# Softmax maxima of the graph attention passes: cut into three bfloat16 parts and picked with bfloat16 one-hots

## The chip, the cores and the metric

One core of one Trainium2 chip runs the whole program. The metric is the device time of one execution in microseconds (us), the lower the better. TensorE (PE; its weight loads are listed apart as PEld) multiplies, VectorE (DVE) and ScalarE (ACT) do elementwise work, GpSimd (POOL) issues the indirect gathers, and SyncE (SP) issues the plain transfers.

## What is computed

The reference runs four graph networks over the same 3,125 nodes and 103,125 edges, each followed by a residual and a layer norm. The change touches only the third, a diffusion network with three graph attention ("gat") layers. Cut to what matters:

```
for gw, a_s, a_d, gb, aw, ab, g, b in layers:          # 3 layers, 8 heads, width 256, 256, 128
    xw     = (x @ gw).reshape(n, 8, c)
    al_s   = einsum(xw, a_s);  al_d = einsum(xw, a_d)   # per node and head
    logits = leaky_relu(al_s[src] + al_d[dst], 0.2)
    m      = segment_max(logits, dst)                   # per node and head
    e      = exp(logits - m[dst])
    out    = segment_sum(e / segment_sum(e, dst)[dst] * xw[src], dst)
```

## The kernel before

**Tiling.** The edges are sorted by destination and cut into groups of 512 edges that share one block of 128 destination nodes. Two groups make a step: 8 items (`BATCH`) of 128 edges. A gat layer is one `gat_pass` of 114 steps, so there are 342 steps in three layers. Each engine runs its own loop over the steps, four steps to a turn of the loop (`pipeline`); a pair such as `(2, logits)` says that a part works two steps behind. Nothing but this list sets the order on an engine, and semaphores join the engines.

**One step, in the order of its data.** POOL gathers the source rows of the step's edges with 8 indirect transfers (L681); its gather of step n waits for the messages of step n-4. ACT takes al_s out of them (`pack`), PE transposes it (`turn`, L1795), DVE scans for the running maxima of each run of equal destinations (`scan`, L1683), and PE transposes back (`turn_back`, L1801). DVE's `run_ends` (L1690) keeps the maxima at the end of each run and zeros the rest, and ACT puts the flag of a run's end beside them. PE's `pick` (L1811) multiplies these 9 columns by the one-hot matrix of the edges' destinations, one matmul for each of 8 items, in float32: since each destination has one run in an item, the product picks its maximum. DVE's `maxima` (L1700 to L1729) makes the new maximum of each node of the block, cuts it into three bfloat16 parts whose sum is the float32 number, and PE's `dst_gather` (L1824) brings al_d and the maximum to the edges with 24 bfloat16 matmuls of 16 columns (8 items by 3 parts). This document calls that group the burst. DVE's `logits` (L1735, L1738, L1741) and ACT's `power` (L1669) make the exponentials, DVE's `messages` (L1748) multiplies the gathered rows by them, PE's `sums` (L1834, in two halves, float32) adds up the messages by destination, and DVE's `add` (L1768, L1772) adds them to the accumulator.

**Around the change.** The one-hots arrive from memory in bfloat16 (`hot_half`, a ring of 4 that SP loads, L709), and ACT widens them to float32 (`hot`, L719); `pick` and `sums` read the float32 ones. DVE's list for a turn is `maxima` (two behind), `scan` (one behind), `logits` (two), `run_ends` (one), `keep_fade` (two), `add(0)` (three), `messages` (two), `add(1)` (three). So DVE reaches the messages of one step only after `run_ends` of the next. PE's list is `turn` (one), `sums(0)` (three), `dst_gather` (two), `turn_back` (one), `sums(1)` (three), `pick` (one).

## Time and profile before

| | before |
|---|---|
| Median of 3 runs | 11818.08 us (11797.62 to 11822.92) |
| Time of the profiled execution | 11901.01 us |
| Its span, first to last instruction | 11899.2 us |
| Busy: PE, PEld | 6783.1 us (57%), 5699.3 us (48%) |
| Busy: POOL, DVE, ACT | 6085.0 (51%), 4232.3 (36%), 1966.8 us (17%) |
| Mean granted TensorE clock | 0.616 of full speed |
| gat layers 0, 1, 2 (first to last L1735) | 4617.5 to 6426.2, 6554.9 to 8354.9, 8481.9 to 10191.6 us |

The profiled execution took 83 us (0.7%) more than the median of the plain runs, and every duration below is from it. No engine is busy for 60% of the span. The three gat passes are 5.3 of the 11.9 ms.

In a timeline row the first number is the start in us from the span's start and the second the length; then come engine, line, operation, what it writes and reads, and the number of instructions that are merged in the row. In brackets stands the idle time of the engine just before it and what ended it; "remote" and "issue" mean that the profile names no instruction. One float32 matmul of the program is two MATMUL records, a bfloat16 one is one.

### The profile page before, as it was taken

What the parts mean: (1) busy time and instruction counts of PE and PEld (TensorE: products, weight loads), DVE (VectorE), ACT (ScalarE), POOL (GpSimd) and SP (SyncE); (2) the same over time, 40 slices, a digit from 0 to 9 for tenths busy, and PEclk for the clock granted to TensorE, in tenths of its full rate; (3) what the DMA queues carried; (4) which work ended last, traced back from release to release, by engine and by line L of the source; (5) the groups of instructions that cost most, each with busy time, mean ns of one, the idle gap of its engine ahead of it and who ended that gap; (6) DMA issues with size and microseconds to landing.
All of it is one profiled execution on the core that took longest, in us unless ns stands there. A gap on an engine that the chain in (4) does not pass through costs nothing. (4 is left out here: it accounts for less than half of the span.)

```text
span 11899.2 us, 136950 instructions
## 1 busy us (share of the span) xinstructions
PE 6783.1 (57%) x37299; PEld 5699.3 (48%) x37300; DVE 4232.3 (36%) x12350; ACT 1966.8 (17%) x5277; POOL 6085.0 (51%) x6396
## 2 busy tenths in 40 slices
PE   3554555556444445666666666676555555545454
PEld 3554544455322324555555555555455555444444
DVE  4333322222211113444444444444334333333333
ACT  1222200001211121111112111111211111111111
POOL 4666656665466653444443444444344444355554
PEclk6555556555667666666666666666655555566566
DMA  4444423232233322333332333333222222233333
GB/s 122 142 140 137 134 68 78 76 78 63 73 73 74 74 70 88 103 103 103 103 103 87 103 104 104 104 104 102 63 74 76 75 75 75 60 95 95 96 94 83
DMA packets 774628, 1092.78 MB, mean 92 GB/s; under 512 B 389184, under 2 KB 429440, under 8 KB 774160
## 3 DMA queue, kind: packets, MB, share of 16 engines
q0 software_dynamic: 233760, 503.07, 17.3%
q1 hardware_dynamic: 540784, 588.70, 16.5%
q8 instruction: 40, 0.66, 0.0%
q14 instruction: 44, 0.36, 0.0%
HBM read 1016.16 MB, written 75.04 MB: 92 GB/s over the span
## 5 line engine op out<-in xcount | busy, mean ns | idle before, releaser
L681 POOL DMA_INDIRECT gat_rows<-xw_table,gat_index x2736 | 2592.0, 947 | 3118.1 <-DVE gat_msg_s L1748 1971.9
L1834 PE MATMUL bank<-gat_msg_s,gat_hot 128*128 128x264 f32 (+1 forms) x5472 | 1942.7, 528 | 28.6 <-DVE gat_msg_s L1748 16.3
L1811 PE MATMUL bank<-gat_ends_s,gat_hot 128*128 128x9 f32 x5472 | 1153.2, 350 | 1183.1 <-issue 857.8
L1811 PEld LDWEIGHTS bank<-gat_ends_s,gat_hot 128*128 128x128 f32 x5472 | 1137.0, 316 | 1319.8 <-issue 950.0
L1834 PEld LDWEIGHTS bank<-gat_msg_s,gat_hot 128*128 128x128 f32 x5472 | 1430.8, 303 | 296.3 <-issue 31.0
L681 POOL DMA_INDIRECT att_rows<-pre_table,att_index x912 | 862.5, 946 | 830.1 <-ACT att_index L671 478.9
L681 POOL DMA_INDIRECT msg_rows<-pre_table,msg_index x912 | 864.8, 948 | 651.0 <-ACT msg_index L671 385.1
L681 POOL DMA_INDIRECT gcn_rows<-in_x,gcn_index x912 | 878.6, 963 | 573.8 <-ACT gcn_index L671 291.1
L681 POOL DMA_INDIRECT gcn_rows<-x_table,gcn_index x912 | 883.4, 969 | 554.4 <-issue 278.9
L893 PE MATMUL bank<-gcn_rel,gcn_rhot 100*128 100x64 f32 x3648 | 705.7, 347 | 792.4 <-issue 608.1
L730 PE MATMUL bank<-gcn_msg_s,gcn_hot 128*128 128x128 f32 x3648 | 844.9, 379 | 538.0 <-issue 530.4
L893 PEld LDWEIGHTS bank<-gcn_rel,gcn_rhot 100*128 100x128 f32 x3648 | 682.9, 271 | 821.9 <-issue 758.2
L730 PEld LDWEIGHTS bank<-gcn_msg_s,gcn_hot 128*128 128x128 f32 x3648 | 728.1, 281 | 620.8 <-issue 619.6
L1735 DVE TENSOR_TENSOR gat_lg<-gat_al_s,bank 128x64 f32<-128x64 f32 x342 | 75.7, 221 | 1957.9 <-remote 1924.1
L1748 DVE TENSOR_TENSOR gat_msg_s<-gat_rows,bank 128x2112 f32<-128x2112 f32 (+1 forms) x342 | 681.3, 1992 | 0.4
L1824 PE MATMUL bank<-gat_parts,gat_dhot 128*128 128x16 bf16 x8208 | 265.2, 172 | 687.8 <-DVE gat_parts L1729 386.0
L1824 PEld LDWEIGHTS bank<-gat_parts,gat_dhot 128*128 128x128 bf16 x8208 | 243.9, 101 | 857.5 <-issue 856.7
L1259 PE MATMUL bank<-msg_w,msg_attr_t 128*128 128x512 f32 x456 | 346.6, 903 | 397.0 <-ACT msg_attr_t L1169 231.9
L1205 DVE TENSOR_TENSOR msg_pre_s<-msg_rows,bank 128x512 f32<-128x512 f32 x228 | 146.5, 684 | 1167.0 <-DMA gcn_hot_half<-edge_hots 1051.7
L861 DVE TENSOR_TENSOR bank<-gcn_rows,bank 128x512 f32<-128x512 f32 x228 | 157.6, 691 | 1101.8 <-remote 720.6
L1669 ACT ACTIVATE bank<-gat_lg 128x64 f32<-128x64 f32 x342 | 77.9, 228 | 2485.6 <-DVE gat_lg L1741 1841.6
L730 PE MATMUL bank<-msg_msg_s,msg_hot 128*128 128x129 f32 x1824 | 288.5, 301 | 309.9 <-issue 309.5
(279 smaller groups left out, 8925.6 us busy)
## 6 DMA issues: line engine op xcount, KB each, us to landing
gcn_ids<-rel_rows SPq DMA_DIRECT2D x228, 400.0 KB
gat_hot_half<-edge_hots SPq DMA_DIRECT2D x342, 256.0 KB
gat_dhot<-dst_hots SPq DMA_DIRECT2D x342, 256.0 KB
gcn_dst<-dst_rows SPq DMA_DIRECT2D x114, 512.0 KB
gat_rows<-xw_table,gat_index POOLq DMA_INDIRECT x2736
edge_hots<-gcn_hot_half SPq DMA_DIRECT2D x114, 256.0 KB
dst_hots<-gcn_dhot SPq DMA_DIRECT2D x114, 256.0 KB
gcn_hot_half<-edge_hots SPq DMA_DIRECT2D x114, 256.0 KB
```

The lines of the kernel that those rows point to most:

```text
L681: pool.indirect_dma_start(self.rows[n.q][:, j, :], None, self.table, bass.IndirectOffsetOnAxis(ap=self.index[n.q][:, j:j + 1], axis=0))\
L730: ins = pe.matmul(place(banks, g, width), hot[:, g * GROUP + j, :], msg[:, g * GROUP + j, 0:width], start=j == 0, stop=j == GROUP - 1)
L861: dve.tensor_tensor(comp[q], g.rows[n.q][:, :, :], rel_ps[q][:, :].rearrange("p (b d) -> p b d", b=BATCH), ALU.mult)\
L893: ins = pe.matmul(rel_ps[q][:, j * DIM:(j + 1) * DIM], rhot[q][:, j * P:(j + 1) * P], rel[:, :], start=True, stop=True)
L1205: ins = dve.tensor_tensor(pre[q][:, part, :], g.rows[n.q][:, part, :], edge_ps[q][i][:, :].rearrange("p (j d) -> p j d", j=GROUP), ALU.add)
L1259: ins = pe.matmul(edge_ps[q][i][:, :], attr_t[q][:, i * P:(i + 1) * P], w[:, :], start=True, stop=True)
L1669: act.activation(powers, lg[q][:, :, :], ACT.Exp).then_inc(powered, 1)
L1735: dve.tensor_tensor(lg[q][:, :, :], al_s[q][:, :, :], drow[:, :, 0:HEADS], ALU.add)\
L1748: dve.tensor_tensor(msg[q][:, :, :].rearrange("p b (h e) -> p b h e", h=HEADS), rows[n.q][:, :, 0:wide].rearrange("p b (h e) -> p b h e", ...
L1811: ins = pe.matmul(pick_ps[:, j * (HEADS + 1):(j + 1) * (HEADS + 1)], hot[n.q][:, j, :], ends[q][:, j, :], start=True, stop=True)
L1824: ins = pe.matmul(row_ps[:, j * size:(j + 1) * size], dhot[n.q][:, j * P:(j + 1) * P], parts[q][:, j // GROUP, k, :], start=k == 0, stop=k ...
L1834: ins = pe.matmul(sum_ps[g][:, 0:wide], hot[n.q][:, g * GROUP + j, :], msg[q][:, g * GROUP + j, :], start=j == 0, stop=j == GROUP - 1)
```

## The change

`run_ends` is followed on DVE by a new part, `cut_ends`, which cuts the 9 columns of the run ends (8 maxima and the flag) into three bfloat16 parts whose sum is the float32 number. The first part needs no instruction: it is the upper half of each float32 word, read in place. `pick` then makes three bfloat16 matmuls for each item, with the bfloat16 one-hots as they came from memory, and adds them up in PSUM. It no longer waits for ACT's widening, but for the one-hots' landing and for the cut. SP's load of new one-hots now also waits until the pick four steps before is done, and the presets of the semaphore `picked` go from 2 to 4 with the waits shifted to match.

```diff
@@ scalar and vector
-                    dve.wait_ge(picked, n.total(1, 1))
+                    dve.wait_ge(picked, n.total(1, RING - TWO + 1))
                     dve.tensor_tensor(ends[q][:, :, 0:HEADS], back_ps[:, 0:ROWS].rearrange("p (b h) -> p b h", b=BATCH),
                                       spread(m.run_end[:, n.items()], HEADS), ALU.mult).then_inc(masked, 1)
+
+                def cut_ends(n):
+                    q = n.of(TWO)
+                    dve.wait_ge(masked, n.total(1, 2))
+                    dve.wait_ge(flagged, n.total(1, 1))
+                    dve.tensor_tensor(ends_rest[q][:, :, :], ends[q][:, :, :], upper(ends[q][:, :, :]), ALU.subtract).then_inc(ends_cut, 1)
+                    dve.wait_ge(ends_cut, n.total(1, 1))
+                    dve.tensor_tensor(ends_low[q][:, :, :], ends_rest[q][:, :, :], upper(ends_rest[q][:, :, :]), ALU.subtract)\
+                        .then_inc(ends_parted, 1)
...
-                pipeline(dve, (2, maxima), (1, scan), (2, logits), (1, run_ends), (2, keep_fade), (3, add(0)), (2, messages),
+                pipeline(dve, (2, maxima), (1, scan), (2, logits), (1, run_ends), (1, cut_ends), (2, keep_fade), (3, add(0)), (2, messages),
                          (3, add(1)))
@@ tensor
-                    hots.wait(pe, n)
-                    pe.wait_ge(masked, n.total(1, 2))
-                    pe.wait_ge(flagged, n.total(1, 1))
+                    pe.wait_ge(hots.hot_in[n.q], n.count(16, 16))
+                    pe.wait_ge(ends_parted, n.total(1, 1))
                     pe.wait_ge(offered, n.total(1, 1))
+                    pieces = upper(ends[q][:, :, :]), upper(ends_rest[q][:, :, :]), ends_low[q]
                     for j in range(BATCH):
-                        ins = pe.matmul(pick_ps[:, j * (HEADS + 1):(j + 1) * (HEADS + 1)], hot[n.q][:, j, :], ends[q][:, j, :],
-                                        start=True, stop=True)
+                        for k, piece in enumerate(pieces):
+                            ins = pe.matmul(pick_ps[:, j * (HEADS + 1):(j + 1) * (HEADS + 1)], hots.half[n.q][:, j, :], piece[:, j, :],
+                                            start=k == 0, stop=k == PARTS - 1)
                     ins.then_inc(picked, 1)
@@ sync
-                pipeline(sp, (0, hots.load(sp)), (0, load_runs), (0, load_dhot))
+                def load_hots(n):
+                    sp.wait_ge(picked, n.total(1, 1))
+                    hots.load(sp)(n)
+
+                pipeline(sp, (0, load_hots), (0, load_runs), (0, load_dhot))
```

On DVE, between the logits and the messages of a step inside the loop of layer 0, stands before the change:

```order
L1735 TENSOR_TENSOR gat_lg<-gat_al_s,bank 128x64
L1738 SCALAR_TENSOR_TENSOR gat_lg<-gat_lg 128x64
L1741 TENSOR_TENSOR gat_lg<-gat_lg,bank 128x64
L1690 ISA
L1690 TENSOR_TENSOR gat_ends_s<-bank,run_end 128x8x8
L1756 COPY bank<-gat_fade 128x16
L1768 ISA
L1768 TENSOR_TENSOR acc<-acc,bank 128x264
L1770 REGISTER_ALU
L1772 TENSOR_TENSOR acc<-acc,bank 128x264
L1748 TENSOR_TENSOR gat_msg_s<-gat_rows,bank 128x2112
```

And at the same place of the changed kernel, whose line numbers are some 6 to 16 higher (L1750 is `logits`, L1696 `run_ends`, L1763 `messages`):

```order
L1750 TENSOR_TENSOR gat_lg<-gat_al_s,bank 128x64
L1753 SCALAR_TENSOR_TENSOR gat_lg<-gat_lg 128x64
L1756 TENSOR_TENSOR gat_lg<-gat_lg,bank 128x64
L1696 ISA
L1696 TENSOR_TENSOR gat_ends_s<-bank,run_end 128x8x8
L1703 TENSOR_TENSOR gat_ends_rest<-gat_ends_s 128x72
L1705 TENSOR_TENSOR gat_ends_low<-gat_ends_rest 128x72
L1771 COPY bank<-gat_fade 128x16
L1783 ISA
L1783 TENSOR_TENSOR acc<-acc,bank 128x264
L1785 REGISTER_ALU
L1787 TENSOR_TENSOR acc<-acc,bank 128x264
```

The two subtractions over 72 elements a partition (L1703, L1705) are new; the rest keeps its order.

On PE, the end of a step in the loop of layer 0 and the start of the next, before the change:

```order
L1824 MATMUL bank<-gat_parts,gat_dhot 128x16 x24
L1799 REGISTER_ALU
L1801 MATMUL bank<-ident,gat_run_max 128x64
L1832 REGISTER_ALU
L1834 MATMUL bank<-gat_msg_s,gat_hot 128x264 x4
L1807 REGISTER_ALU
L1811 MATMUL bank<-gat_ends_s,gat_hot 128x9 x8
L1795 MATMUL bank<-ident,gat_al_s 64x128
```

In the changed kernel the eight float32 matmuls of L1811 are 24 bfloat16 ones (L1827); the first six of them, behind the sums:

```order
L1850 MATMUL bank<-gat_msg_s,gat_hot 128x264 x4
L1827 MATMUL bank<-gat_ends_s,gat_hot_half 128x9
L1827 MATMUL bank<-gat_ends_rest,gat_hot_half 128x9
L1827 MATMUL bank<-gat_ends_low,gat_hot_half 128x9
L1827 MATMUL bank<-gat_ends_s,gat_hot_half 128x9
L1827 MATMUL bank<-gat_ends_rest,gat_hot_half 128x9
L1827 MATMUL bank<-gat_ends_low,gat_hot_half 128x9
```

Their place among the other groups of PE is the same.

## Rows read from the trace of the kernel before

**Rows 1.** Groups of the page: busy, mean ns | idle before, releaser.

```profile
L1811 PE MATMUL bank<-gat_ends_s,gat_hot 128*128 128x9 f32 x5472 | 1153.2, 350 | 1183.1 <-issue 857.8
...
L1735 DVE TENSOR_TENSOR gat_lg<-gat_al_s,bank 128x64 f32<-128x64 f32 x342 | 75.7, 221 | 1957.9 <-remote 1924.1
```

**Rows 2.** Line L1735 in gat layers 0 and 2.

```profile
L1735 DVE TENSOR_TENSOR gat_lg<-gat_al_s,bank x114: 220/222/222, 4617.5 to 6426.2; 128x64 f32<-128x64 f32 x114
...
L1735 DVE TENSOR_TENSOR gat_lg<-gat_al_s,bank x114: 220/222/223, 8481.9 to 10191.6; 128x64 f32<-128x64 f32 x114
```

**Rows 3.** Timeline, one step, layer 0: start, length, engine, line [idle, releaser].

```profile
5216.64 0.22 DVE L1735 TENSOR_TENSOR gat_lg<-gat_al_s,bank 128x64 f32<-128x64 f32 x1 [7.00 <-remote]
5216.90 0.23 DVE L1738 SCALAR_TENSOR_TENSOR gat_lg<-gat_lg 128x64 f32<-128x64 f32 x1
...
5217.35 0.23 DVE L1690 TENSOR_TENSOR gat_ends_s<-bank,run_end 128x64 f32<-128x64 f32 x1
...
5217.67 3.56 PE L1811 MATMUL bank<-gat_ends_s,gat_hot 128*128 128x9 f32 x16 [3.88 <-issue]
...
5218.48 2.35 DVE L1748 TENSOR_TENSOR gat_msg_s<-gat_rows,bank 128x2112 f32<-128x2112 f32 x1
...
5221.27 3.73 PE L1834 MATMUL bank<-gat_msg_s,gat_hot 128*128 128x264 f32 x8
5221.60 0.95 POOL L681 DMA_INDIRECT gat_rows<-xw_table,gat_index  x1 [6.71 <-DVE gat_msg_s L1748]
...
5226.10 0.75 PE L1824 MATMUL bank<-gat_parts,gat_dhot 128*128 128x16 bf16 x24 [1.09 <-issue]
...
5230.36 0.94 POOL L681 DMA_INDIRECT gat_rows<-xw_table,gat_index  x1 [0.30 <-issue]
...
5233.12 0.22 DVE L1735 TENSOR_TENSOR gat_lg<-gat_al_s,bank 128x64 f32<-128x64 f32 x1 [6.70 <-remote]
```

**Rows 4.** Timeline, another step of layer 0.

```profile
5463.70 0.95 POOL L681 DMA_INDIRECT gat_rows<-xw_table,gat_index  x1 [6.69 <-DVE gat_msg_s L1748]
...
5467.14 0.76 PE L1824 MATMUL bank<-gat_parts,gat_dhot 128*128 128x16 bf16 x24
...
5472.48 0.95 POOL L681 DMA_INDIRECT gat_rows<-xw_table,gat_index  x1 [0.30 <-issue]
...
5473.73 0.22 DVE L1735 TENSOR_TENSOR gat_lg<-gat_al_s,bank 128x64 f32<-128x64 f32 x1 [6.51 <-remote]
```

**Rows 5.** Timeline, one step of layer 2.

```profile
9096.73 0.95 POOL L681 DMA_INDIRECT gat_rows<-xw_table,gat_index  x1 [5.40 <-DVE gat_msg_s L1748]
...
9097.73 0.17 DVE L1700 TENSOR_SCALAR gat_pen<-bank 128x8 f32<-128x8 f32 x1 [1.17 <-PE bank L1811]
...
9101.08 0.79 PE L1824 MATMUL bank<-gat_parts,gat_dhot 128*128 128x16 bf16 x24 [1.32 <-issue]
...
9105.49 0.95 POOL L681 DMA_INDIRECT gat_rows<-xw_table,gat_index  x1 [0.30 <-issue]
...
9108.28 0.22 DVE L1735 TENSOR_TENSOR gat_lg<-gat_al_s,bank 128x64 f32<-128x64 f32 x1 [7.16 <-remote]
```

**Rows 6.** What L1700 waited for, us and times: layer 0, then layer 2.

```profile
  PE bank L1811: 18.0, 11
...
  PE bank L1811: 138.0, 104
```

**Rows 7.** Timeline, layer 0: a burst with no gather under way.

```profile
5585.86 0.79 PE L1824 MATMUL bank<-gat_parts,gat_dhot 128*128 128x16 bf16 x24 [12.81 <-DVE gat_parts L1729]
...
5586.69 0.22 DVE L1735 TENSOR_TENSOR gat_lg<-gat_al_s,bank 128x64 f32<-128x64 f32 x1 [0.75 <-PE bank L1824]
```

**Rows 8.** Attention pass: its bfloat16 burst, and the windows view of it.

```profile
10819.13 1.49 PE L2133 MATMUL bank<-q_parts,att_dhot 128*128 x24
...
10820.75 0.69 DVE L2073 TENSOR_TENSOR att_prod<-att_rows,bank 128x512 f32<-128x512 f32 x1 [0.67 <-PE bank L2133]
...
10819.10:10820.70 1.60, 1.60 (x28) 1.57 (x26) 0.70 (x1) 0.00 (x0) 0.94 (x1) 0.50 0.65 178
```

More of the change, by code:

```diff
@@ L1595, in gat_pass @@
         turned, scanned, backed, masked, flagged, picked = (st.sem(s) for s in ("turned", "scanned", "backed", "masked", "flagged", "picked"))
+        ends_cut, ends_parted = st.sem("ends_cut"), st.sem("ends_parted")
         penal, offered, best, shown, sloped, local = (st.sem(s) for s in ("penal", "offered", "best", "shown", "sloped", "local"))
@@ L1603, in gat_pass @@
         runs, run_max = ring_sb(st, "runs", RING, [ROWS, P]), ring_sb(st, "run_max", TWO, [ROWS, P])
-        ends = ring_sb(st, "ends_s", TWO, [P, BATCH, HEADS + 1])
+        ends, ends_rest = (ring_sb(st, s, TWO, [P, BATCH, HEADS + 1]) for s in ("ends_s", "ends_rest"))
+        ends_low = ring_sb(st, "ends_low", TWO, [P, BATCH, HEADS + 1], BF16)
         pen, cand = ring_sb(st, "pen", TWO, [P, BATCH]), ring_sb(st, "cand", TWO, [P, BATCH, HEADS])
@@ L1649, in bring @@
                     ins.then_inc(shown, 1)
-                    act.wait_ge(picked, n.total(1, 1))
+                    act.wait_ge(picked, n.total(1, RING - TWO + 1))
                     act.activation(ends[q][:, :, HEADS:HEADS + 1], m.run_end[:, n.items()].unsqueeze(2), ACT.Copy).then_inc(flagged, 1)
@@ L1698, in maxima @@
                     earlier[:], ids = ids[:-PAIR], ids[-PAIR:]
-                    dve.wait_ge(picked, n.total(1, TWO + 1))
+                    dve.wait_ge(picked, n.total(1, RING + 1))
                     dve.tensor_scalar(pen[q][:, :].unsqueeze(2), view[:, :, HEADS:HEADS + 1], -1.0, -FAR, ALU.add, ALU.mult)\
@@ L1840, in _ @@
                 pe.sem_inc(backed, TWO)
-                pe.sem_inc(picked, TWO)
+                pe.sem_inc(picked, RING)
                 pe.sem_inc(dst_rows, RING)
```

## The prediction

> **What bounds the kernel now.** I read the groups of the page first, to see what waits. `logits` (L1735) on DVE waits 1957.9 us over 342 steps, 1924.1 of it for "remote", a releaser that the profile cannot name [rows 1]. `pick` (L1811), which the change rebuilds, is busy for 1153.2 us on PE [rows 1]: much work, but work on an engine that is idle four tenths of the time. So the question is whether any wait ends with it.
>
> The steps of the three layers are compared by the first and last start of L1735: 113 intervals in (6426.2 − 4617.5) / 113 = 16.01 us in layer 0 and (10191.6 − 8481.9) / 113 = 15.13 us in layer 2 [rows 2].
>
> Then the timeline of one step [rows 3]. L1735 starts at 5216.64 (call it R), the messages at 5218.48 and end at 5220.83. POOL, which waited for them, starts its first gather at 5221.60, 0.77 later, and ends the eighth at 5230.36 + 0.94 = 5231.30. The next L1735 starts at 5233.12. The loop is logits, run ends, add, messages, eight gathers, logits: 1.84 + 2.35 + 0.77 + 9.70 + 1.82 = 16.48 us. DVE has hardly a gap between L1735 and L1748, so that is a chain of DVE work, without cover.
>
> Why do logits wait for the gathers? They need only `dst_gather` (L1824, the burst), which is recorded from 5226.10 to 5226.85, 6.3 us before they start [rows 3]. In another step, where the burst starts 5467.14 − 5463.70 = 3.44 us after the first gather, logits start 5473.73 − 5473.43 = 0.30 after the end of the last one [rows 4]. In rows 3 it starts 4.50 after the first gather and logits come 1.82 after the last. In layer 2 it is 9101.08 − 9096.73 = 4.35, and 9108.28 − 9106.44 = 1.84 [rows 5]. With no gather under way a burst ending at 5586.65 releases logits at 5586.69 [rows 7]; and in the attention pass a burst of the same 24 matmuls, 1.49 us long, hands on at once while the DMA engines are 65% busy [rows 8]. I read this so: a completion of PE's that falls late enough among the gathers is seen only when they have drained, and 0.30 or 1.8 us behind the last is decided by where the burst starts, with the border between 3.44 and 4.35 us after the first gather. That is an inference from few rows; the sum rests on it.
>
> `pick` runs from R + 1.03 to R + 4.59, before the first gather at R + 4.96 [rows 3]. What reads it is L1700, the start of the maxima. It waits for the pick in 11 steps of layer 0, 18.0 us in all, but in 104 steps of layer 2, 138.0 us [rows 6]: there the messages are half as wide, so DVE arrives before PE.
>
> **The change, part by part.** *Added on DVE's path: two subtractions a step.* Each depends on the one before it. L1735 and L1738 are such a pair, of 64 elements, and start 0.26 apart [rows 3]; for 72 elements I take the same. So 2 × 0.26 = 0.52 us a step, 342 steps, **+178 us**. The next instruction keeps its distance, and messages, gathers and logits all start 0.52 later: nothing covers it. Lower bound: the 0.17 us that the smallest operation lasts (L1700, rows 5), 2 × 0.17 × 342 = +116. Upper bound: a hand-over between engines, 5217.67 − 5217.35 = 0.32 from L1690 to the pick [rows 3], 2 × 0.32 × 342 = +219. I stay near the pair of dependent operations, the same kind of thing.
>
> *Taken from PE: the pick.* Sixteen float32 records take 3.56 us; 24 bfloat16 ones take 0.75 in the burst of the same step [rows 3]. The new pick starts after two cuts, at about R + 1.5, and ends near R + 2.3, some 2.3 us earlier. In layers 0 and 1 it ends before DVE is done with the messages (R + 4.19) either way, or nearly: only the 18.0 us of waits can go [rows 6], and I allow as much again for layer 1. Between 0 and −36, taken **−20 us**. PE's sums start 5221.27 after the old pick's end at 5221.23; they may now start 0.4 earlier, but PE then idles 1.09 before the burst in any case [rows 3]: nothing.
>
> In layer 2 the wait of L1700 was 1.17 in rows 5. Of it some 0.2 would remain between two dependent starts of DVE, so the maxima and the burst come about 0.96 earlier, at 9100.12, 3.39 after the first gather instead of 4.35. That is just on the early side of the one early row I have (3.44), so the release may go from 1.84 to 0.30 behind the last gather, 1.54 a step. None of 114 steps gives 0, all give −176. As the new place is so near the border, and as not all of the 138.0 us need be gone (a wait of DVE's own may stand behind it), I take half: 57 × 1.54 = **−88 us**. A step that stays late gains nothing, since its release hangs on the last gather.
>
> *Moved.* The pick no longer waits for ACT's widening, but for the one-hots' landing four steps ahead; SP's load of one-hots waits for the pick of four steps before instead of for the widening. Behind it in SP's queue stand the loads of runs and of the destination one-hots. The latter already waits for `dst_rows`, that is, for a burst that is seen as late as logits see it, so the added wait, for an earlier event of an earlier step, ends first: 0. The flag of ACT, a step old by then: 0.
>
> Sum: 178 − 20 − 88 = **+70 us** against the profiled execution's 11901.01; scaled by 11818.08 / 11901.01 it is +70 again on the median, **11,888 us**. Bounds: 116 − 36 − 176 = −96 and +219, so 11,722 to 12,037.
>
> **A colder TensorE?** PE's granted clock is 0.50, its lower level of 1.2 GHz, beside the short attention burst [rows 8], and the sums of rows 3 take 3.73 us and still end at 5225.00, 1.09 before the burst. So a PE that is half as fast in its sums costs nothing there. The Trainium skill, "TensorE: Matmul & The Clock Gate", section "HAM oscillation — how this bites in real kernels", says that gaps in TensorE's work send it back to half rate, which speaks against making PE idler; the rows agree that PE works at half rate here and give no cost for it.
>
> **The rivals.**
> *A, faster.* Every step of layer 2 falls on the early side. Place: the start of the burst after the first gather; it decides from the border on, if that is at 3.4 us or above. Then −176, and with all 36 us and cuts at 0.21 (+145): −67, **11,750 us**. For it: 3.39 is below 3.44. Against: by 0.05, and only if nothing else delays L1700. Chance 0.28.
> *B, no change.* The cuts near 0.26 and layer 2 nearly all early, or the cuts lighter and half of it early: 150 − 150, **11,818 us**. Also here: the cuts turn out to be covered, which would need a gap in DVE's chain from R to the messages, and I see none. Chance 0.20.
> *C, far slower.* A completion of the pick itself, now a burst of bfloat16 matmuls, is held like the other until the gathers are over, and the maxima with it. It would need the pick to fall among the gathers; it ends 2.6 us before them. In irregular steps it might: a step then grows by up to a further round of about 5 us (half the 9.70 of the gathers), in one of ten steps 34 × 5 = +170, and with the cuts **12,150 us**. Or the sums grow past their margin of 1.09. Chance 0.08.
> *The forecast:* cuts in full, layer 2 partly repaid: 11,845 to 12,000. Chance 0.44.
>
> **How the numbers follow.** ±0.2% of 11818, that is 11,794 to 11,842, is about what a measurement of this kernel can tell from no change. Slower: forecast and C, 0.52. Within: B, 0.20. Faster: A, 0.28. The predicted time is the forecast's, 11,888. Its own range is 11,845 to 12,000. The whole range, 11,730 to 12,010, leaves out C (0.08), the cuts at their upper bound with no repayment (some 0.06) and the last of A (0.05).
>
> **What would show it.** The starts of the two cuts (L1703, L1705) 0.26 apart, and messages (L1763) 2.36 after L1750 in layer 0 rather than 1.84. L1827 as 24 records in about 0.8 us, ended before the first gather. L1715 in layer 2 with hardly a wait for PE. L1840 there at 3.4 us after the first gather in all steps, and L1750 at 0.30 behind the last gather in half of them, 1.8 in the other half. Mean steps of 16.01 + 0.52 − 0.1 = 16.4 in layer 0 and 15.13 + 0.52 − 0.77 = 14.9 us in layer 2. Wrong it would be if the release did not depend on the burst's place: then no −88, and 11,976. And if the earlier pick moved more than L1700, as when the order of POOL's gathers relative to the burst changes in layers 0 and 1 as well, where each step that turns early gives 1.5 us, 228 steps up to 350.

## The result and the profile after

The changed kernel took 11904.87 us (median of 4 runs, 11880.46 to 11928.7), the kernel before on the same chip 11815.43 us. The ratio is 1.0082, 95% interval 1.0065 to 1.0099: slower, by 77 to 117 us. The forecast was 11,888 us, +70.

The groups of the page of the changed kernel that answer to [rows 1]:

```profile
L1827 PE MATMUL bank<-gat_ends_s,gat_hot_half 128*128 128x9 bf16 x2736 | 250.6, 169 | 1289.2 <-issue 1289.2
...
L1750 DVE TENSOR_TENSOR gat_lg<-gat_al_s,bank 128x64 f32<-128x64 f32 x342 | 75.7, 221 | 1897.2 <-remote 1836.4
```

There are three such groups of L1827. Their matmuls overlap in time, so their busy times are not to be added: together they cover 269 us, where L1811 took 1153.2. TensorE as a whole is busy 805 us less (5978.4 against 6783.1). The wait of the logits for "remote" is 1836.4 us, 88 less than before. So 805 us of work left the engine, and the kernel became slower.

Line L1750 in gat layers 0 and 2 (first and last start), beside [rows 2]:

```profile
L1750 DVE TENSOR_TENSOR gat_lg<-gat_al_s,bank x114: 220/222/223, 4577.5 to 6397.6; 128x64 f32<-128x64 f32 x114
...
L1750 DVE TENSOR_TENSOR gat_lg<-gat_al_s,bank x114: 220/222/223, 8482.5 to 10193.6; 128x64 f32<-128x64 f32 x114
```

(6397.6 - 4577.5) / 113 = 16.11 us a step in layer 0, and 15.14 in layer 2. The prediction had put 16.4 and 14.9 there. The profile of before is very likely of an execution on a slower chip (see "The kernel before again" below), so small differences to [rows 2] are not to be read by themselves.

The timeline of one step of layer 0, changed kernel, beside [rows 3]. Of the 24 rows of the pick the first and the last are shown:

```profile
5305.68 0.22 DVE L1750 TENSOR_TENSOR gat_lg<-gat_al_s,bank 128x64 f32<-128x64 f32 x1 [6.38 <-remote]
...
5306.38 0.22 DVE L1696 TENSOR_TENSOR gat_ends_s<-bank,run_end 128x64 f32<-128x64 f32 x1
5306.64 0.23 DVE L1703 TENSOR_TENSOR gat_ends_rest<-gat_ends_s 128x72 f32<-128x72 f32 x1
5306.91 0.23 DVE L1705 TENSOR_TENSOR gat_ends_low<-gat_ends_rest 128x72 bf16<-128x72 f32 x1
5307.24 0.17 PE L1827 MATMUL bank<-gat_ends_s,gat_hot_half 128*128 128x9 bf16 x1 [2.81 <-issue]
...
5307.83 0.17 PE L1827 MATMUL bank<-gat_ends_low,gat_hot_half 128*128 128x9 bf16 x1
5308.01 2.35 DVE L1763 TENSOR_TENSOR gat_msg_s<-gat_rows,bank 128x2112 f32<-128x2112 f32 x1
...
5311.14 0.94 POOL L681 DMA_INDIRECT gat_rows<-xw_table,gat_index  x1 [5.63 <-DVE gat_msg_s L1763]
...
5315.64 0.75 PE L1840 MATMUL bank<-gat_parts,gat_dhot 128*128 128x16 bf16 x24 [1.26 <-issue]
...
5319.90 0.95 POOL L681 DMA_INDIRECT gat_rows<-xw_table,gat_index  x1 [0.30 <-issue]
5322.42 0.34 SPq L1635 DMA_DIRECT2D gat_dhot<-dst_hots  x1
5322.43 0.22 DVE L1750 TENSOR_TENSOR gat_lg<-gat_al_s,bank 128x64 f32<-128x64 f32 x1 [6.47 <-remote]
```

The cuts stand 0.27 apart and behind `run_ends`; the messages start 2.33 after L1750, not 1.84. The pick takes 0.76 us and is over before the messages start. The burst is 4.50 behind the first gather and the logits 5322.43 - 5320.85 = 1.58 behind the last one. So messages and gathers take over the whole 0.5 us. The step as a whole is 0.27 us longer than the one in [rows 3] (16.75 against 16.48), since there the logits came 1.82 behind the last gather.

The row of SyncE (SPq, L1635) bears on the main open point. SyncE's load of new destination one-hots waits for the same semaphore (`dst_rows`) as the logits, and it goes on at 5322.42, 0.01 us before them, 6.03 us behind the burst's recorded end (5316.39). Two engines see it late at the same moment, so it is the completion that comes late, and VectorE is not what delays it.

The same rows in layer 2, for a step with an early burst, beside [rows 5]:

```profile
9097.99 0.95 POOL L681 DMA_INDIRECT gat_rows<-xw_table,gat_index  x1 [5.87 <-DVE gat_msg_s L1763]
9098.03 0.17 DVE L1715 TENSOR_SCALAR gat_pen<-bank 128x8 f32<-128x8 f32 x1 [0.21 <-issue]
...
9101.32 0.79 PE L1840 MATMUL bank<-gat_parts,gat_dhot 128*128 128x16 bf16 x24 [1.79 <-DVE gat_parts L1744]
...
9106.75 0.94 POOL L681 DMA_INDIRECT gat_rows<-xw_table,gat_index  x1 [0.30 <-issue]
9108.81 0.22 DVE L1750 TENSOR_TENSOR gat_lg<-gat_al_s,bank 128x64 f32<-128x64 f32 x1 [7.42 <-remote]
```

What L1715, the start of the maxima, waited for in layer 2, in us and times, beside [rows 6]:

```profile
  DMA edge_hots<-gcn_hot_half: 68.1, 9
  issue: 62.8, 101
```

In the regular steps the wait for the pick is gone: 62.8 us remain in 101 steps, where it was 138.0 in 104. The burst is 9101.32 - 9097.99 = 3.33 us behind the first gather, as forecast (3.39), but the logits follow the last gather's end by 9108.81 - 9107.69 = 1.12 us, not 0.30.

The other nine waits are of another kind, and the releaser that the profile names for them is not a fitting one, since L1715 waits for the semaphore `picked` alone. About once in twelve steps the gathers of two steps stand close together, in layer 2 fifteen in a row, and the pick falls among them. One of the nine:

```profile
8844.06 0.17 DVE L1715 TENSOR_SCALAR gat_pen<-bank 128x8 f32<-128x8 f32 x1 [8.26 <-DMA edge_hots<-gcn_hot_half]
```

The pick had ended at 8828.00 by its record, 16.06 us earlier, with gathers running until 8841.21. So this is rival C of the prediction, in irregular steps. Over all three layers the maxima's idle time grew from 443.3 to 473.7 us, though its part for the pick (164.1 us before) is gone; the part with the unfitting name rose from 120.7 to 311.2. It did not cost time of its own: such a pair of steps took 10.8 + 21.7 = 32.5 or 12.2 + 20.4 = 32.6 us in layer 2 before, and takes 9.8 + 22.7 = 32.5 now. The kernel before had the same pairs, and there the longest wait stood at L1772 (10.79 us for "remote" in one of them).

For every step whose eight gathers stand in a row, the burst's start behind the first gather and the logits' start behind the end of the last can be counted from the same rows. Layer 2 has 92 such steps in each kernel:

| | burst behind first gather | steps | logits behind the last gather's end |
|---|---|---|---|
| before | 4.3 to 4.4 | 80 | 1.7 to 1.9 in 78, 0.3 and 1.0 in one each |
| before | 4.0, 4.2, 4.7, 5.6 | 12 | 1.7 to 1.8 in all |
| after | 3.3 to 3.4 | 45 | 1.0 to 1.1 in 22, 1.7 in 7, 0.3 in 6, before its end in 10 |
| after | 4.0 | 19 | 1.7 in 15, 0.2 to 1.0 in 4 |
| after | 4.5 | 27 | 1.7 to 1.9 in all |
| after | 2.5 | 1 | before its end |

On average the logits came 1.74 us behind the last gather before and come 1.08 behind it now. In layers 0 and 1 of the changed kernel a burst at 3.4 to 3.7 was released at 0.3 us behind the last gather or earlier in 88 of 90 steps, and one at 4.5 at 1.5 to 1.7 in all 52; at 4.1 to 4.2 both kinds stand side by side.

### The profile page after: what moved, and what is told of

It is laid out like the page before. It is cut to its first block and busy times, and to the rows that moved or that the text cites. A ratio compares the mean times of both kernels' runs of the same rounds, so it can differ in the third digit from the quotient of the medians.

```text
span 11878.7 us, 143529 instructions
## 1 busy us (share of the span) xinstructions
PE 5978.4 (50%) x40035; PEld 4797.1 (40%) x40036; DVE 4377.9 (37%) x13034; ACT 1967.9 (17%) x5277; POOL 6086.8 (51%) x6396
## 5 line engine op out<-in xcount | busy, mean ns | idle before, releaser
L1850 PE MATMUL bank<-gat_msg_s,gat_hot 128*128 128x264 f32 (+1 forms) x5472 | 2031.9, 541 | 628.4 <-DVE gat_msg_s L1763 479.7
L730 PE MATMUL bank<-gcn_msg_s,gcn_hot 128*128 128x128 f32 x3648 | 796.0, 369 | 421.3 <-issue 415.7
L1827 PE MATMUL bank<-gat_ends_s,gat_hot_half 128*128 128x9 bf16 x2736 | 250.6, 169 | 1289.2 <-issue 1289.2
L730 PEld LDWEIGHTS bank<-gcn_msg_s,gcn_hot 128*128 128x128 f32 x3648 | 695.3, 273 | 480.5 <-issue 480.1
L1827 PEld LDWEIGHTS bank<-gat_ends_s,gat_hot_half 128*128 128x128 bf16 x2736 | 230.2, 104 | 1425.1 <-issue 1422.5
L1750 DVE TENSOR_TENSOR gat_lg<-gat_al_s,bank 128x64 f32<-128x64 f32 x342 | 75.7, 221 | 1897.2 <-remote 1836.4
L1763 DVE TENSOR_TENSOR gat_msg_s<-gat_rows,bank 128x2112 f32<-128x2112 f32 (+1 forms) x342 | 681.4, 1992 | 0.2 <-issue 0.2
L1259 PE MATMUL bank<-msg_w,msg_attr_t 128*128 128x512 f32 x456 | 302.3, 799 | 457.6 <-ACT msg_attr_t L1169 353.4
L730 PE MATMUL bank<-att_msg_s,att_hot 128*128 128x64 f32 x1824 | 343.7, 344 | 178.8 <-issue 175.2
```

The lines of the kernel that those rows point to most:

```text
L730: ins = pe.matmul(place(banks, g, width), hot[:, g * GROUP + j, :], msg[:, g * GROUP + j, 0:width], start=j == 0, stop=j == GROUP - 1)
L1259: ins = pe.matmul(edge_ps[q][i][:, :], attr_t[q][:, i * P:(i + 1) * P], w[:, :], start=True, stop=True)
L1750: dve.tensor_tensor(lg[q][:, :, :], al_s[q][:, :, :], drow[:, :, 0:HEADS], ALU.add)\
L1763: dve.tensor_tensor(msg[q][:, :, :].rearrange("p b (h e) -> p b h e", h=HEADS), rows[n.q][:, :, 0:wide].rearrange("p b (h e) -> p b h e", ...
L1827: ins = pe.matmul(pick_ps[:, j * (HEADS + 1):(j + 1) * (HEADS + 1)], hots.half[n.q][:, j, :], piece[:, j, :], start=k == 0, stop=k == PART ...
L1850: ins = pe.matmul(sum_ps[g][:, 0:wide], hot[n.q][:, g * GROUP + j, :], msg[q][:, g * GROUP + j, :], start=j == 0, stop=j == GROUP - 1)
```

## The experiments

Each ratio is to the kernel before, run on the same chip. The runs did not all fall on one chip: on most the kernel before took 11,815 to 11,920 us, on one 8,795. Of the kernel before there are two profiles, and both are, the first very likely, from a chip where it takes about 11,920.

**One part alone: the cuts.** The kernel before with the two subtractions, which nobody reads:

```diff
-pipeline(dve, ..., (2, logits), (1, run_ends), (2, keep_fade), ...
+pipeline(dve, ..., (2, logits), (1, run_ends), (1, cut_ends), (2, keep_fade), ...
```

> The kernel before with the two subtractions added, their results read by nobody; the pick stays float32. My theory (two dependent DVE operations cost 2 x 0.26 us a step on the path, nothing comes back): 342 x 0.52 = +178 us, ratio 1.015 (1.012 to 1.018), slower than the changed kernel. Rival (a subtraction is cheap, and the changed kernel's +0.8% is all there is, the new pick giving nothing back): +90 us, ratio 1.008. Rival (half-step releases are a lottery that a shift of half a us can turn either way): anything from 1.00 to 1.02, with the starts of L1735 behind the last gather showing another mix of 0.3 and 1.8 us than in the kernel before.

Measured 1.0093 (1.0078 to 1.0109), 11923.98 against 11817.4 us: +107. The starts in layers 0 and 2:

```profile
L1746 DVE TENSOR_TENSOR gat_lg<-gat_al_s,bank x114: 220/221/223, 4586.9 to 6422.0; 128x64 f32<-128x64 f32 x114
...
L1746 DVE TENSOR_TENSOR gat_lg<-gat_al_s,bank x114: 220/221/222, 8518.8 to 10233.2; 128x64 f32<-128x64 f32 x114
```

That is 16.24 and 15.17 us a step. In layer 2 L1711, the maxima, still waits for the pick 104 times:

```profile
  PE bank L1822: 104.3, 104
```

The first theory (+178) misses. The +90 of the second lies within the interval, but its reason does not hold: the two subtractions stand 0.27 us apart here as well, and the pick does give something back (next run). The third, the mix of releases, is what is seen: in layer 2 the pick does not move with the cuts, only messages and gathers do, so the burst falls 3.8 to 4.0 us behind the first gather instead of 4.3, and 37 of 54 such steps are released at 0.1 to 0.3. The 0.5 us is nearly paid back there: the layer takes 1714.4 us, against 1709.7 and 1711.5 in the two profiles of the kernel before.

**The other part alone: the pick.** The changed kernel without the cuts; the pick multiplies the upper halves and twice a tile of zeros, which leaves out the lower bits of the maxima:

```diff
-                    pe.wait_ge(ends_parted, n.total(1, 1))
+                    pe.wait_ge(masked, n.total(1, 2))
+                    pe.wait_ge(flagged, n.total(1, 1))
-                    pieces = upper(ends[q][:, :, :]), upper(ends_rest[q][:, :, :]), ends_low[q]
+                    pieces = upper(ends[q][:, :, :]), none, none
```

> The changed kernel without the two subtractions: the pick is three bfloat16 matmuls an item, of the upper halves and of twice a tile of zeros, so the maxima lose their lower bits. My theory (the short pick lets the maxima of layer 2 start earlier, and some steps are then released 0.3 instead of 1.8 us behind the last gather): -60 to -180 us, ratio 0.985 to 0.995. Rival (the short pick gives nothing, the cut is worth only +90): ratio 1.000.

Measured 0.9977 (0.9968 to 0.9986): -25 us. It gains, but a quarter of what I had forecast. Against it the changed kernel is 112 us slower by the medians. Of the two profiled executions it is 92 us slower, and its three gat layers, first to last logits of each, are 5351.9 - 5239.2 = 113 us longer: all that the cuts cost lies there.

The two profiles also show how it splits. In layers 0 and 1 it is 29 and 30 us, 0.26 a step: the logits come on average 1.00 and 0.98 us behind the last gather in pick_only and 0.76 and 0.72 in the changed kernel, so a quarter of a us comes back by a better mix of releases. In layer 2 it is 53 us, 0.47 a step; there the mix gets a little worse (0.93, then 1.08). And the parts are not independent: on top of the cuts the short pick is worth 11923.98 - 11904.87 = 19 us, of which 3 us in layer 2, where the cuts alone had already won most of the early releases.

What is an early release worth? In layer 2 of pick_only the messages start 3.40 us behind the last gather's end where the logits came 1.5 to 1.9 behind it (31 steps), 2.79 where they came at 0.9 to 1.2 (27 steps), and 2.49 where they came at 0 to 0.4 (28 steps). So 0.6 and 0.9 us, not 1.54. One of the last kind:

```profile
8470.93 0.69 PE L1807 MATMUL bank<-ident,gat_run_max 64*128 64x64 f32 x2
8475.55 0.94 POOL L681 DMA_INDIRECT gat_rows<-xw_table,gat_index  x1 [0.30 <-issue]
8476.78 0.22 DVE L1740 TENSOR_TENSOR gat_lg<-gat_al_s,bank 128x64 f32<-128x64 f32 x1 [6.40 <-remote]
8478.34 0.23 DVE L1695 TENSOR_TENSOR gat_ends_s<-bank,run_end 128x64 f32<-128x64 f32 x1 [0.82 <-DMA msg_te_b<-in_L_gnn_te_b]
```

The logits (L1740) come 0.29 behind the last gather's end (8476.49). But `run_ends` (L1695), which stands between them and the messages, reads `turn_back` (L1807), which PE had ended at 8471.62, and it starts only 1.85 behind that gather. (The releaser that the profile names for it is not a tensor of this pass.) It waits over 0.3 us in 20 of those 28 steps and in none of the other 58. So here the burst's completion is early and the next one of PE is still late, and half of the gain is lost again.

**A wait more on POOL.** To test why the logits are late, the gathers are held back until the burst is done:

```diff
             for j in range(BATCH):
+                if after is not None and j == 0:
+                    pool.wait_ge(after, n.total(1, 2))
+                    pool.sem_inc(self.passed, 1)
...
-                gather.program(pool, msg_made)
+                gather.program(pool, msg_made, dst_rows)
```

> The changed kernel, whose POOL in the gat passes waits for one thing more: the gathers of a step start only when the burst (dst_gather) of the step three before has completed. My theory (a completion of PE's that falls among gathers is seen only when they have drained): gathers that start right behind one burst are over, or nearly, when the next one ends some 9.3 us later, so a step falls from 16 to between 10.3 and 12 us in all three layers: -1100 to -1950 us, ratio 0.84 to 0.91, though it only adds a wait. Rival (logits wait for the gathers themselves, or for their rows, or DMA is the bound): the gathers start 4 to 5 us later in each step and nothing is gained, ratio 1.00 to 1.13, steps of 16 to 20 us.

Measured 0.9894 (0.9879 to 0.9909), steps of 15.1 us. A step's timeline:

```profile
5287.20 0.95 POOL L684 DMA_INDIRECT gat_rows<-xw_table,gat_index  x1 [6.40 <-PE bank L1843]
...
5291.29 0.17 PE L1830 MATMUL bank<-gat_ends_low,gat_hot_half 128*128 128x9 bf16 x1
...
5295.96 0.95 POOL L684 DMA_INDIRECT gat_rows<-xw_table,gat_index  x1 [0.30 <-issue]
5297.13 0.17 DVE L1718 TENSOR_SCALAR gat_pen<-bank 128x8 f32<-128x8 f32 x1 [5.05 <-DMA edge_hots<-gcn_hot_half]
5300.47 0.79 PE L1843 MATMUL bank<-gat_parts,gat_dhot 128*128 128x16 bf16 x24 [6.43 <-DVE gat_parts L1747]
5301.30 0.22 DVE L1753 TENSOR_TENSOR gat_lg<-gat_al_s,bank 128x64 f32<-128x64 f32 x1 [0.66 <-PE bank L1843]
```

The logits now follow the burst at once (5301.26, 5301.30). But the pick, ended at 5291.46 among the gathers, is seen by the maxima at 5297.13, 0.22 behind the last gather's end. The wait has moved from the burst to the pick. That is rival C of the prediction, now in every regular step. So a wait more makes the kernel faster, by far less than the 1100 us expected: I had counted one completion of PE's, and there are two in a step that DVE waits for.

**The cuts behind the messages.** One entry of DVE's list is moved:

```diff
-(1, run_ends), (1, cut_ends), (2, keep_fade), (3, add(0)), (2, messages), (3, add(1))
+(1, run_ends), (2, keep_fade), (3, add(0)), (2, messages), (1, cut_ends), (3, add(1))
```

> The changed kernel with the two subtractions behind the messages in DVE's list. The messages come 0.52 us earlier again, the pick ends at about R + 5.5 in layers 0 and 1, with the first gather at R + 5.0. My theory (the cuts before the messages are what costs; a completion within the first 3 us of the gathers is not held): -100 to -180 us against the changed kernel, less what the maxima lose by waiting some 0.4 us for the pick: ratio to the kernel before 0.993 to 1.002. Rival C of the prediction (the completion of the bfloat16 pick is held like the burst's once it falls among the gathers): the maxima wait up to 9 us more, ratio 1.15 or more.

Measured 1.0127 (1.0111 to 1.0142), slower than the changed kernel, where I had expected 0.993 to 1.002. A step's timeline:

```profile
5321.97 0.22 DVE L1750 TENSOR_TENSOR gat_lg<-gat_al_s,bank 128x64 f32<-128x64 f32 x1 [6.27 <-remote]
...
5326.93 0.94 POOL L681 DMA_INDIRECT gat_rows<-xw_table,gat_index  x1 [7.06 <-DVE gat_msg_s L1763]
...
5327.28 0.17 PE L1827 MATMUL bank<-gat_ends_low,gat_hot_half 128*128 128x9 bf16 x1
...
5328.97 0.17 DVE L1715 TENSOR_SCALAR gat_pen<-bank 128x8 f32<-128x8 f32 x1 [1.50 <-PE bank L1827]
...
5332.28 0.75 PE L1840 MATMUL bank<-gat_parts,gat_dhot 128*128 128x16 bf16 x24 [1.06 <-issue]
...
5335.67 0.95 POOL L681 DMA_INDIRECT gat_rows<-xw_table,gat_index  x1 [0.30 <-issue]
5338.60 0.22 DVE L1750 TENSOR_TENSOR gat_lg<-gat_al_s,bank 128x64 f32<-128x64 f32 x1 [6.24 <-remote]
```

The messages start at R + 1.83, 0.5 us earlier, as meant. But the pick ends half a us into the gathers, the maxima (L1715) start 5328.97 - 5327.45 = 1.52 us behind its end, at R + 7.0, the burst falls 5.35 behind the first gather, and the logits come 1.98 behind the last gather instead of 0.2 to 1.6. So "early among the gathers is not held" is wrong too: it is late by 1.5 us (the median of each layer is 1.52 or 1.53), not by all of the gathers.

**The kernel before again,** for a second profile:

> The kernel before, unchanged, for a second profile of it, since the first is of an execution 0.7% above the median. If the layers differ only by how often a step is released 0.3 or 1.7 us behind the last gather: the three gat layers together some 50 us shorter than the 5318 us of the first profile, with the same kinds of steps in another mix. Rival (the first one lost its time outside the gat layers): the gat layers again 5318 us, the rest 80 us shorter.

On this chip it took 11919.64 us (median), and the gat layers 5347 us: neither expectation. Outside of the gat layers this profile has 6582 us and the first one 6581, while the profiles from chips where the kernel before takes 11,815 to 11,820 have 6513 to 6547, and the other three from this chip 6555 to 6571. So the first profile's 11901.01 is very likely of such a chip as this, and not of a slow execution.

**The same wait in the kernel before** (edit as in after_wait):

> The kernel before, whose gathers of a step start only behind the burst of the step three before, as in after_wait; the pick stays float32. My theory (a completion of PE's among running gathers is seen when they have drained; with this wait it is no longer the burst that is held but the pick): the pick is among the gathers either way, whether it takes 3.6 or 0.8 us, and is seen behind the last gather; steps of 14.4 to 16.3 us, the ratio to the kernel before 0.980 to 0.990, a little below after_wait by the two cuts. Rival (the pick is late in after_wait for another reason, and a float32 pick is later by its own 2.8 us): ratio 1.02 to 1.06.

Measured 0.9496 (0.948 to 0.9512), far below what I expected; steps of 14.2 and 13.6 us. The maxima wait for the pick here too, and often start at R + 9.4, before the last gather ends. With the float32 pick the wait takes 5.0% off its kernel, with the bfloat16 one 1.9% (0.9894 / 1.0082). The two ran on different chips. Why a pick that ends later is seen earlier is open.

**Two pauses instead of one.** Five gathers wait for the pick, three for the burst:

```diff
+            if first is not None:
+                pool.wait_ge(first, n.total(1, 2))
             pool.wait_ge(used, n.total(1, 1))
...
+                if rest is not None and j == 5:
+                    pool.wait_ge(rest, n.total(1, 2))
+                    pool.sem_inc(self.passed, 1)
```

> The changed kernel with the eight gathers of a step in two groups: five wait for the pick of the step three before (and for the messages, as now), three for the burst of that step. So POOL pauses at both places at which DVE waits for PE. My theory: the pick ends at R + 5.0, after the three gathers (R + 0.8 to R + 4.5) have drained, and is seen at once; the five gathers run from R + 5.6 to R + 11.8, and the burst, done at R + 9.7, is seen 0.2 to 1.7 behind them: steps of 12.0 to 13.5 us in place of 16, ratio 0.89 to 0.93. Rival (gathers only have to be done, wherever they stand; or a pause costs what it frees): steps of 15 to 17, ratio 0.97 to 1.03.

Measured 0.9303 (0.9288 to 0.9319), 11087.03 us: steps of 13.4 us. A step's timeline:

```profile
5328.16 0.22 DVE L1755 TENSOR_TENSOR gat_lg<-gat_al_s,bank 128x64 f32<-128x64 f32 x1 [4.45 <-remote]
...
5334.10 0.94 POOL L686 DMA_INDIRECT gat_rows<-xw_table,gat_index  x1 [1.74 <-DMA edge_hots<-gcn_hot_half]
5334.89 0.17 DVE L1720 TENSOR_SCALAR gat_pen<-bank 128x8 f32<-128x8 f32 x1 [1.18 <-issue]
...
5338.15 0.78 PE L1845 MATMUL bank<-gat_parts,gat_dhot 128*128 128x16 bf16 x24 [1.30 <-issue]
5339.10 0.94 POOL L686 DMA_INDIRECT gat_rows<-xw_table,gat_index  x1 [0.30 <-issue]
5341.59 0.22 DVE L1755 TENSOR_TENSOR gat_lg<-gat_al_s,bank 128x64 f32<-128x64 f32 x1 [3.17 <-remote]
```

The pick no longer delays the maxima, and the burst, done at 5338.93, is seen 1.55 behind the last gather's end. The long steps are gone too: none takes over 16.6 us, where the changed kernel has nine of 21 to 23 us in each layer. The work is that of the changed kernel, in 0.9303 / 1.0082 = 0.923 of its time: where the gathers stand decides. It beats both kernels.

**Pick first, additions one step later,** with the wait of after_wait (PE's list ends `(1, pick), (3, sums(1))`, DVE's has `(4, add(1)), (3, add(0))` ahead of the messages):

> As after_wait, and besides PE does the pick before the second half of the sums, and DVE does the second addition of a step one step later, before the first addition and the messages of the next. So the pick ends at R + 2.5, 1.7 us behind the start of the gathers, and the additions no longer stand before the maxima. My theory (only completions that fall late among the gathers are held): the pick is seen at once, the maxima start at R + 5.6, the burst ends at R + 9.7 and is seen 0.2 to 1.7 us behind the last gather's end at R + 10.5: steps of 10.7 to 12.3 us, ratio 0.85 to 0.90. Rival (every completion among gathers is held, early or late): the maxima start at R + 10.7 or later again, steps of 15 to 16, ratio 0.98 to 1.01.

Measured 0.9508 (0.9492 to 0.9524), steps of 14.2 and 13.9 us, between theory and rival. In its timeline the pick ends 1.7 us into the gathers, and the maxima start 6.9 us later:

```profile
5317.20 0.94 POOL L684 DMA_INDIRECT gat_rows<-xw_table,gat_index  x1 [5.84 <-PE bank L1844]
...
5318.73 0.17 PE L1831 MATMUL bank<-gat_ends_low,gat_hot_half 128*128 128x9 bf16 x1
...
5325.81 0.17 DVE L1722 TENSOR_SCALAR gat_pen<-bank 128x8 f32<-128x8 f32 x1 [3.41 <-DMA edge_hots<-gcn_hot_half]
5325.94 0.94 POOL L684 DMA_INDIRECT gat_rows<-xw_table,gat_index  x1 [0.30 <-issue]
```

The maxima started before the last gather had, so "only when they have drained" does not hold either.

**Plain copies for the gathers,** which leave out the gathering (the first 1024 rows of the table each time):

> The kernel before, whose eight indirect gathers of a gat step are eight plain copies of as many rows each (always the first 1024 rows of the table, so the gathered values are other ones), issued by POOL and waited for in the same places. If what delays PE's completions is the indirect gathers themselves: no burst is seen late any more, L1735 starts behind the burst, at some R + 9.3 to R + 10.5, ratio 0.80 to 0.88. Rival (it is the traffic of the rows, or of all transfers, 11 KB a partition and step, whoever describes it): PE's completions are late as before, ratio 0.97 to 1.02. Rival (POOL's issuing of any transfer is what holds them): the same as the second, with POOL busy as now.

This fell on the chip on which the kernel before takes 8794.81 us, and measured 0.9965 (0.9952 to 0.9977). A step's timeline:

```profile
4708.65 0.75 PE L1827 MATMUL bank<-gat_parts,gat_dhot 128*128 128x16 bf16 x24 [1.86 <-issue]
4709.44 0.22 DVE L1738 TENSOR_TENSOR gat_lg<-gat_al_s,bank 128x64 f32<-128x64 f32 x1 [0.46 <-PE bank L1827]
```

The logits follow the burst at once, steps are 10.2 us. But the kernel before, with its indirect gathers, is within 0.4% of it on this chip. The passes that the edit left alone, whose gathers are still indirect, show the same. In the first network (gcn) ACT's widening of the one-hots waits for PE's sums. The group of the page in the kernel before, and then here:

```profile
L719 ACT ACTIVATE gcn_hot<-gcn_hot_half 128x1024 f32<-128x1024 bf16 x114 | 120.6, 1058 | 1245.9 <-remote 1025.1 <-issue 115.8 <-PE bank L730 97.1
...
L722 ACT ACTIVATE gcn_hot<-gcn_hot_half 128x1024 f32<-128x1024 bf16 x114 | 120.4, 1057 | 1005.5 <-PE bank L733 996.6 <-DMA gcn_hot_half<-edge_hots 8.9
```

Here the widening starts 0.04 to 0.10 us behind PE's recorded end, in 112 of 114 cases with gathers running. On the other chips its wait is mostly for "remote". And not only completions are late there. PE stops between two matmuls of one group, though no wait stands between them in the program. A row of the kernel before, and one of the same line here:

```profile
508.69 0.27 PE L893 MATMUL bank<-gcn_rel,gcn_rhot 100*128 100x64 f32 x1 [2.60 <-issue]
...
504.39 2.26 PE L896 MATMUL bank<-gcn_rel,gcn_rhot 100*128 100x64 f32 x16
```

In the first 3000 us there are 651 such stops of over 0.7 us in the kernel before, 938 us in all, and 585 to 656 in the other profiles from such chips; here, and in b_two_53 below, there are 6, 35 us in all. So on this chip indirect gathers held up nothing that these traces show, and on the others they, or something beside them, hold up TensorE itself. Whether plain copies would help there is not answered.

**Two groups in the kernel before,** five and three, and four and four:

> As two_groups (five gathers for the pick, three for the burst), but made of the kernel before: float32 pick, no cuts. My theory (what sets a step is now logits, messages or pick, five gathers, the burst seen 0.2 to 1.7 behind them; the float32 pick ends at R + 4.6, hardly after the messages at R + 4.2, and the cuts stand before the messages): each step 0.5 to 0.8 us shorter than in two_groups, so steps of 12.6 to 12.9, ratio 0.91 to 0.92. Rival (the short pick is worth its 2.8 us once the gathers no longer set the step): ratio 0.94 to 0.98, slower than two_groups.

> As b_two_53, with four gathers behind the pick and four behind the burst. The pick ends at R + 4.6 among the four gathers of R + 0.8 to R + 5.7. My theory: it is seen at R + 5.9 at the earliest, four gathers end at R + 11, the burst ends at R + 10.0 and is seen at R + 11.2 to R + 12.6: steps of 11.2 to 12.6 us, ratio 0.87 to 0.91. Rival (a pick that falls among gathers is held up to 7 us, as in before_wait, whatever their number): steps of 13 to 16, ratio 0.93 to 1.0.

Both had a flaw of mine: the semaphore `picked` begins two lower in the kernel before, so the gathers waited for a pick two steps later than meant, and their landing came onto the path. On the same chip they measured 1.489 both, steps of 23.5 us in layer 0. In b_two_53 all waits for PE carry its name, no "remote" is left. They say nothing on the two picks. Mended (`n.total(1, 0)`):

> b_two_53 mended: there the five gathers waited for a pick two steps too late (the semaphore of the kernel before begins two lower), here for that of the step three before, as in two_groups; otherwise the kernel before with its float32 pick and no cuts. On a chip on which the kernel before takes 11.8 to 11.9 ms: steps of 12.6 to 12.9 us and a ratio of 0.91 to 0.92 if the cuts before the messages (0.52 us a step) are what separates it from two_groups (0.930); 0.94 to 0.98 if the short pick was worth more than they. On a chip like the one of b_two_53, where the kernel before takes 8.8 ms and no burst is seen late, the pauses can only cost: gathers that end at R + 11 leave rows late, ratio 1.0 to 1.15.

Measured 0.924 (0.9227 to 0.9252), 10923.41 us, on a chip where the kernel before takes 11819.67; steps of 12.98 and 12.90 us. Ratio and steps are just above what I expected. Against the kernel before of its own chip this is the fastest version. Its ratio is 0.7% below that of two_groups, and its gat layers take 4392 us against 4514, on different chips. So with the waits moved too, the float32 pick without cuts is the better one.

## Why the prediction was right, and where its sizes were off

**The cuts are on the path, without cover: right, the term too large.** They stand 0.27 apart and delay the messages by 0.5 us in every step, as forecast. Their net cost was 107 us in cuts_only and 112 on top of pick_only, not 178, and below even the lower bound of 116. The sum left out that the cuts also move the gathers against the burst and so change the mix of releases. In cuts_only that paid back nearly all of layer 2; in the changed kernel against pick_only it paid back half of layers 0 and 1 and nothing of layer 2.

**The short pick frees layer 2: right in kind, the term too large.** The waits for the pick are gone from the regular steps, and the burst comes at 3.3 to 3.4 us in 45 of 92, not in all. There the release is mostly at 1.0 to 1.1, which the two places of the forecast (0.30 and 1.8) did not have: the reading "just on the early side of the one early row I have" rested on a row of layer 0. And the price of 1.54 for an early release was too high for the 0.3 ones as well: it prices the logits, but the messages wait for `run_ends`, and that for another completion of PE's. In pick_only the messages gained 0.6 to 0.9 us. Measured were -25 us (pick_only), against -108 for both terms. Layer 2 of pick_only takes 1657.9 us against 1709.7 and 1711.5 in the profiles of the kernel before, 52 to 54 less; where the other 27 went can't be told without a profile of the kernel before from the same chip.

**The sum.** +107 - 25 = +82, measured +89; forecast +178 - 108 = +70. Two terms, 71 and 83 us too large, cancelled, so it is luck that the sum came so near. The places show it: the steps were to be 16.4 us in layer 0 and 14.9 in layer 2, and are 16.11 and 15.14. The sign was no luck: the cuts alone cost 107 us, four times what the pick alone gave. What was added was in a chain without gaps, what was taken away was mostly work beside it.

**The border between 3.44 and 4.35** held in layers 0 and 1 of the changed kernel, but not everywhere: in pick_only 12 of the 58 bursts at 3.4 to 3.5 in these layers were released at 1.7 to 1.9. The reading behind it, that a completion of PE's is seen when the gathers have drained, is too simple. Gaps in the gathers at the places where DVE waits for PE took 7% off, but the delay is sometimes 1.5 us (cut_late) and sometimes ends before the last gather (reordered). Two completions of the same step can be released at different places (pick_only).

**Moved waits.** SP's later load of one-hots and ACT's flag cost nothing that a run shows; no run tests them alone, but pick_only has both and is faster than the kernel before. The colder clock: the mean granted clock is 0.616 before and after, so nothing of the +89 us is seen to come from it.

**Rival C** did not come true in the regular steps of the change, since the pick ends before the gathers. It came true in nine steps of each layer, where the pick falls among the gathers, but cost nothing there, since before the change those steps had a wait of the same kind at another place. In after_wait and cut_late it came true in the regular steps as well.

## What to carry to other kernels

Work taken from an engine that waits four tenths of its time buys only the steps in which another waits for it, here 25 us for 805 us of work; two small operations put into a gapless chain cost every step. Before costing an edit, look for waits whose releaser the profile cannot name, and see what else is under way then: here the place of the gathers, not the amount of work, was worth 7%. When a delay moves all but one party of a race, price the race as well as the delay. And price an earlier release at the instruction that matters (here the messages), since the next wait may take half of it back.

## What was not expected of the hardware

While GpSimd issues indirect gathers, a completion of TensorE's is seen by other engines long after its recorded end: 6.9 us for the pick in reordered (5318.90 to 5325.81), 16 us in the irregular steps of the changed kernel (8828.00 to 8844.06). VectorE, SyncE and, in the first network, ScalarE all see it late. In that network TensorE also stops for some 2 us between matmuls with no wait between them. (The recorded ends of matmuls are modelled, so part of the delay may lie in the matmuls.) On the other chip the kernel before took 8795 instead of 11,815 to 11,920 us, 26% less, and the traces of plain_rows and b_two_53, taken there, show none of this, though indirect gathers run in both. That is one chip at one time; whether it is the chip or its condition then is not shown. The runs don't settle what holds TensorE up, whether it is the issue of the gathers or their traffic, why it depends on the chip, or what decides between the releases 0.3, 1.0 and 1.7 us behind the last gather.
